# Adding layer 0's bias to the node features by transfers in memory instead of by a matmul in each chunk

## What is computed

```python
h = jnp.maximum(_layernorm(x, axis=-1), 0.0)
x = x + _L0_gnn_ref(h, src, dst, W, b)          # relu(A_norm @ h) @ W.T + b
h = jnp.maximum(_layernorm(x, axis=-1), 0.0)
x = x + _L1_gnn_ref(h, ...)                     # messages with edge types, then a GRU cell
```

## Time and profile before

| | us |
|---|---|
| median of 3 runs | 916.81 (916.66 to 917.4) |
| the profiled execution: its own time | 916.74 |
| the profiled execution: span of its instructions | 915.0 |
| PE busy | 841.8 (92%) |
| DVE busy | 762.6 (83%) |
| ACT busy | 505.8 (55%) |
| POOL busy | 97.1 (11%) |

### The profile page before, as it was taken

The page is one execution under the profiler, slowest core; times in us unless marked ns, Lnnn a source line. Parts: engine busy times, 40 slices in busy tenths (PEclk is TensorE's granted clock), DMA queues, the critical chain, the costliest instruction groups (busy, mean ns, idle before and its releaser), DMA issues.

```text
span 915.0 us, 20961 instructions
## 1 busy us (share of the span) xinstructions
PE 841.8 (92%) x8962; PEld 753.2 (82%) x8962; DVE 762.6 (83%) x934; ACT 505.8 (55%) x940; POOL 97.1 (11%) x86
## 2 busy tenths in 40 slices
PE   2344899999999999999999999999999999999996
PEld 2233788889888888988989888989889888988985
DVE  4987999999999999999999981568766766766886
ACT  3678688888888888888888883211111111111011
POOL 6569202001030020000000000000000000000000
PEclk9999999999999999999999999999999999999999
DMA  4540434346443355443345410497667667667750
GB/s 106 148 168 23 167 147 172 154 179 237 183 174 154 153 205 213 183 163 147 153 180 212 185 30 13 171 293 276 241 254 293 228 246 294 247 228 287 266 207 20
DMA packets 37995, 169.19 MB, mean 185 GB/s; under 512 B 7841, under 2 KB 21036, under 8 KB 34952
## 3 DMA queue, kind: packets, MB, share of 16 engines
q1 hardware_dynamic: 31898, 159.98, 46.5%
q0 software_dynamic: 5664, 6.52, 2.6%
q10 hardware_dynamic: 334, 1.29, 0.5%
HBM read 87.72 MB, written 79.74 MB: 183 GB/s over the span
## 4 chain that ended last, share of the span: by engine, by line
PE 79%; ACT 8%; DVE 6%; POOL 3%; issue 2%; DMA 1%; DVEq 0%; ACTq 0%
PE ps L1357 29%; PE ps L1215 23%; PE ps L1204 14%; ACT ring L1000 6%; POOL tab L525 3%; DVE work L758 2%; PE ps L1241 2%; DVE work L765 1%; PE ps L1227 1%; PE ps L1309 1%; PE ps L1312 1%; PE ps L1314 1%; PE ps L1310 1%; PE ps L1311 1%; PE ps L1313 1%
## 5 line engine op out<-in xcount | busy, mean ns | idle before, releaser
L1204 PE MATMUL ps<-work 128*128 128x106 f16 x3125 | 430.1, 215 | 47.3 <-ACT ring L1000 26.6
L1215 PE MATMUL ps<-ring,tab 125*128 125x250 f16 x2500 | 415.3, 271 | 0.7 <-ACT ring L1005 0.7
L1000 ACT ACTIVATE ring<-ps 128x848 f16<-128x848 f32 x375 | 331.2, 885 | 77.6 <-PE ps L1204 71.1
L1204 PEld LDWEIGHTS ps<-work 128*128 128x128 f16 x3125 | 285.3, 100 | 70.7 <-ACT ring L1000 29.2
L1357 PE MATMUL ps<-ring,tab 125*128 125x250 f16 (+1 forms) x2500 | 277.0, 270 | 0.0
L1357 PEld LDWEIGHTS ps<-ring,tab 125*128 125x128 f16 (+1 forms) x2500 | 242.6, 97 | 28.5
L1215 PEld LDWEIGHTS ps<-ring,tab 125*128 125x128 f16 x2500 | 243.4, 98 | 24.3 <-ACT ring L1005 0.9
L758 DVE TENSOR_TENSOR work<-iota_row,mch 128x3906 f16<-128x3906 f16 x100 | 222.6, 2226 | 4.5 <-PE ps L1204 3.9
L765 DVE TENSOR_TENSOR work<-iota_w,mch 128x3100 f16<-128x3100 f16 x100 | 181.4, 1814 | 0.0
L846 DVE TENSOR_TENSOR work<-work,ring 125x3250 f16<-125x3250 f16 (+1 forms) x92 | 161.7, 1780 | 1.2 <-DMA ring<-adjacency 1.2
L1151 ACT ACTIVATE tab<-ps,bg 128x250 f32<-128x250 f32 x25 | 11.7, 469 | 147.7 <-PE ps L1310 146.9
(11 more groups left out here) (191 smaller groups left out, 636.4 us busy)
## 6 DMA issues: line engine op xcount, KB each, us to landing
adjacency<-ring SPq DMA_DIRECT2D x23, 2937.5 KB
ring<-adjacency SPq DMA_DIRECT2D x46, 812.5 KB, 6.5
ring<-adjacency SPq DMA_DIRECT2D x46, 750.0 KB, 9.4
adjacency<-ring SPq DMA_DIRECT2D x23, 183.1 KB
out<-x_sb SPq DMA_DIRECT2D x24, 125.0 KB
h_turned<-hst SPq DMA_DIRECT2D x23, 125.0 KB, 2.0
tab<-h_turned SPq DMA_DIRECT2D x23, 125.0 KB, 2.1
x_sb<-x SPq DMA_DIRECT2D x3, 560.0 KB
```

The costliest lines, as they stand in the source:

```text
L1000: act.activation(to(x * 2 * u, 2, x), ps[:, s:s + 2, 0:x * SLOTS].rearrange("p b (x h) -> p h b x", h=SLOTS), ACT.Copy).then_inc(sem("evac ...
L1204: last = pe.matmul(ps[:, 2 * (u % 2) + i // BANKW, o:o + WCOLS], lohot[:, s, k, :], combo[:, s, k, :], start=True, stop=True)
L1215: mm = pe.matmul(psD[c % 2], tabv[0][P, h, s, :], adj[c % 2][P, h, :], start=i == 0, stop=i == 2 * BLOCKS - 1)
```

## The change

The bias matmul of each chunk (L1229) goes; the two matmuls by `W` now open and close their own accumulation. `split_bias` (eight DVE instructions) and the memset of its tile on POOL go too. In their place POOL issues, when all of `h0` is made, five transfers that add the bias row from memory to `x_sb` in place, ten blocks (1250 pieces of 512 B, 640 KB) at a time. Each of them waits until the one before has landed. They stand in POOL's queue behind the rows of `h0` and ahead of `run_edges(9)` to `run_edges(24)`. DVE's addition of chunk k now also waits for the transfer that covers its blocks: chunks 0 to 4 for the first, 5 to 9 for the second, and so on. ACT's Sign activation writes into another tile.

```diff
@@ gpsimd_main
-            gp.memset(b_parts[:, :, :], 0.0)
...
                 last.then_inc(sem("rows_p"), 1)
+
+            gp.wait_ge(sem("h0"), ON_ACT)
+            gp.wait_ge(sem("rows_v"), TBATCHES - ON_ACT - ON_POOL)
+            gp.wait_ge(sem("rows_p"), ON_POOL)
+            for t in range(XP):
+                positive(gp, sem("biased"), 16 * t)
+                gp.dma_start(x_sb[P, XB * t:XB * (t + 1), :],
+                             bass.AP(tensor=b0.tensor, offset=b0.offset, ap=[[0, LO], [0, XB], [1, D]]),
+                             accum_op=ALU.add).then_inc(sem("biased"), 16)
             for g in range(3 + RAW, CHUNKS):
                 run_edges(g)
@@ vector_prepare
-            split_bias(v, ch)
@@ post0_x_vector
+            v.wait_ge(sem("biased"), 16 * (CB * k // XB + 1))
             v.wait_ge(sem("psX"), k + 1)
             v.tensor_tensor(x_sb[P, blocks(k), :], psX, x_sb[P, blocks(k), :], ALU.add).then_inc(sem("x1"), 1)
@@ scalar_main
-            act.activation(onesb[:, :], ones[:, 0:LO], ACT.Sign)
+            act.activation(aggr[:, 0:LO], ones[:, 0:LO], ACT.Sign)
@@ post0_x_tensor
-                pe.wait_ge(sem("bias_parts"), 1)
             for j in range(CB):
-                pe.matmul(psX[:, j, :], aggr[:, LO * j:LO * (j + 1)], w0_sb[:, :], start=j == 0, stop=False,
-                          skip_group_check=True)
-            pe.matmul(psX, onesb[0:65, :], b_parts[0:65, :, :], start=False, stop=True, skip_group_check=True)\
-              .then_inc(sem("psX"), 1)
+                last = pe.matmul(psX[:, j, :], aggr[:, LO * j:LO * (j + 1)], w0_sb[:, :], start=True, stop=True)
+            last.then_inc(sem("psX"), 1)
```

More of the change, by code:

```diff
@@ L77 @@
 heads_in weights_in dst_in x_in0 x_in1 x_in2 x_in3 x_in4 ends_set ends_in
-iotas consts consts0 headhots hist totals counted rows_i bias_parts later_in cand_in0 cand_in1 cand_in2 cand_in3 cand_in4 run_i
+iotas consts consts0 headhots hist totals counted rows_i biased later_in cand_in0 cand_in1 cand_in2 cand_in3 cand_in4 run_i
 runs_in0 runs_in1 runs_in2 runs_in3 runs_in4 runs_in5
@@ L191, in gnn @@
         iota_s = sb("iota_s", [128, PAIRS + 1], F16)
-        onesb = sb("onesb", [128, LO], BF16)
-        b_parts = sb("b_parts", [128, CB, D], BF16)
         thr = sb("thr", [128, PAIRS], F32)
@@ L257, in gnn @@
         embf = temps[0:TYPES, :].bitcast(F32)[:, 0:D]
-        bias_high, at = carve(early, at, D)
-        bias_rest, at = carve(early, at, D)
         cand, at = carve(early.bitcast(I32), at, PAIRS, CAND)
@@ L639, in vector_prepare @@
             scale_weights(v, ch)
[L641 to L656, removed]
         def weight_squares(v, ch):
```

## The result

The changed kernel takes **1003.23 us** (1002.62 to 1004.87, four runs) against 917.09 us before it on the same chip (916.66 to 917.4): a ratio of 1.0944, interval 1.093 to 1.0957. That is 86.1 us slower, and far above the range that ended at 945.

The account below looks back on a forecast made before the run. PE and DVE were taken as nearly full in the build loop, PE leading slightly from chunk 3. 916.74 - 2.5 (matmul) - 0 - 0 + 0 = 914.2, median 914.3 us; range 912.8 to 945 us.

Parts of the forecast that it names:

- The matmul: PE's bias matmul removed at 0.11 us per chunk, counted for 23 chunks: 2.5 us saved, between nothing and 3.4.
- Rival 2: DVE holds the build loop, so PE waits for one-hots and nothing is gained: 916.8 us; chance 0.12.
- The splitting: DVE's 2.0 us bias splitting at the start counted as nothing: DVE would wait 3.2 us for first edges instead of 1.2.
- The two deadlines: DVE's chunk 0 addition allows T of 19 us; unpacking chunk 9's edges, fetched behind the fifth transfer, allows about 11.
- T: Time of one bias transfer on POOL's queue from issue to landing, taken as 10.5 us; up to about 11 costs nothing.
- Issuing: POOL's issuing of one 1250-piece transfer: 6.6 us, half of a short fetch's 1.21 us fixed, half growing with pieces.
- Moving the data: Bytes of one transfer, 0.64 MB on 16 engines: about 2.3 us, of which 1 us not covered by issuing.
- low end: Lower bound of one transfer's length: a short fetch's 4.1 us plus 2.3 us for the bytes, 6.4 us.
- High end: Upper bound of one transfer's length: ten times the pieces at POOL's pace, 15.1 us, plus 4.1, 19.2 us.
- Rival 1: Edge fetches come late because issuing 1250 pieces or accumulating is slower: 930 us at T = 15; chance 0.24.
- Rival 3: 125 rows go on 5 engines, bytes take 7.4 us instead of 2.3, T 15.5: 932 us; chance 0.10.
- Rival 4: T above 19.2, perhaps through DVE's traffic, so DVE also stalls in chunk 2: above 947 us; chance 0.06.

Follow-up runs that it names:

- none: Changed kernel without its five transfers and the waits for them, so layer 0's bias is left out of the result: 914.49 us, ratio 0.9973.
- sbuf: Changed kernel with pairs of 112 and 13 rows, three chunks' fetches behind each pair, bias read from its SBUF copy: 914.51 us, ratio 0.9974.
- rowsrc: Changed kernel with pairs of 112 and 13 rows and the bias from SBUF, all fetches still behind the fifth pair: 918.79 us, ratio 1.0019.
- ten: Changed kernel with 112 + 13 rows, fetches moved up, adding ten different pieces of x, each read 125 times, instead of the bias: 913.56 us.
- split: Changed kernel with each transfer cut into a pair of 112 and 13 rows, queue order kept: 967.0 us, ratio 1.0545.
- s125: Changed kernel with only the source moved to the bias copy in SBUF; 125 rows and queue order kept: 991.12 us, ratio 1.0818.
- copy: Changed kernel with three chunks' fetches behind each 125-row transfer, and plain copies overwriting x_sb instead of adding: 937.4 us.
- order: Changed kernel with the edge fetches of three chunks behind each transfer instead of all behind the fifth: 927.76 us, ratio 1.0115.
- both: Changed kernel with pairs of 112 and 13 rows and three chunks' fetches behind each pair, bias still from one memory address: 925.32 us, ratio 1.0079.
- spread: Changed kernel with 112 + 13 rows and fetches moved up, adding 1250 different pieces of x from memory instead of the bias: 913.99 us.

## Why the prediction was wrong

**The matmul: right.** Forecast 2.5 us with the median at 914.3; `none` gave 914.49 and `sbuf` 914.51, so 2.3 and 2.4 us. (The upper bound, 25 x 0.14, is 3.5 us and not 3.4.) The rule used, the distance to the next start and not the 274 ns of the record, is what made it come out. Rival 2, that DVE holds the loop, is out: its waiting for PE shrank from 3.9 to 2.0 us and did not end.

**The splitting: right, as far as it shows.** The 2.3 us are accounted for by the matmul; nothing is left that the splitting would have brought, and in `none` DVE waits the 3.2 us that were forecast.

**The two deadlines: right, and the fetches' place is what costs.** I gave as the rule that from T = 11 us each us costs four. At the 32.0 us that the transfers lay apart that is 4 x (32.0 - 11) = 84 us, and the trace has 75.3, but the two are near each other partly by luck: the terms behind them are off in both directions. The fifth transfer was issued at 220.57 instead of 140, 80.6 us late (my sum had added 7 us for stores, which the 32.0 already hold). Its issuing took 4.0 us and not 6.6. The three fetches took 24.4 us and not 12 to 15. So they landed at 249.0 instead of 159 to 162, 87 to 90 us late. DVE's own need had moved from 159.25 to 248.98 - 75.34 = 173.64, most of it by its first wait of 13.2 us, and 75.3 us are left. One step failed here too: I let DVE be 3.4 us late without loss, and `rowsrc` shows that there is no such room, since its 4.1 us of waiting cost 4.3.

**T: the step that failed.** I bounded T by 6.4 and 19.2 us and took 10.5; it was 25.3 to 34.5. By terms:
- Issuing: reckoned 6.6 us, and 15.1 at the high end; measured 3.63 to 3.82. This was the part I had feared, and it was too high.
- Moving the data: reckoned 2.3 us, of which 1 beside the issuing; measured nearly all of T. The 2.3 us came from POOL's queue, 6.52 MB in 2.6% of the engines' span. But the packets that the trace lists for that queue are of two kinds: those of 4128 and 4608 B carry 6.2 of the 6.52 MB, and nearly all others are of 4 to 16 B. So the rate was that of large packets. One of 4608 B took 231 ns on average, 20 B per ns; one of the 512 B pieces in `ten` took 69 ns, 7.5 B per ns. From the 69 ns, 1250 pieces are 5.4 us of 16 engines' time and 17 of five, an estimate; with rows and source as good as any run had them (`ten`), the data of one pair flowed for 4.6 us, twice the 2.3. The best T seen, 6.8, is just above my low end.
- The two causes that lift it from there are the shared address (T 18.0 to 27.6 in `split`, whose rows are good) and the 125 rows (T 19.7 to 37.2 in `s125`, whose source is good).
- "High end" was therefore no bound: it stretched the issuing tenfold, and left the data at 2.3 us with the same rate and free choice of engines. A bound had to let the dearest unknown, the engines' time for a piece, be as bad as the rows allow, and the earlier trace rows, 5.1 to 10.3 us with the longest beside a store, showed that a store can double it.

**The rivals.** Rival 1 had the right place, the late fetches, and the wrong reasons: issuing was faster than I took it, and adding isn't what makes T long, since `ten` adds as well and lands in 6.8 us. Rival 3, fewer engines, was right in kind and got 0.10, at T = 15.5. The run nearest to it is `s125`: 19.7 us in a clear stretch. It was priced from the same 2.3 us (7.4 us on 5 engines). From the 4.6 us of `ten` it would have been 4.6 x 16 / 5 = 14.7 us of flow, and `s125` has 15.2; that they lie so close is partly luck, since the pair of `sbuf`, which has the source of `s125`, flows for 5.9 us, which would make 18.8.

Against rival 3 I had held that the edge fetches have 125 rows too and land in 5.1 to 10.3 us. They were no evidence against it. The trace doesn't name engines, but it lists each packet's size. The 25 edge fetches before are 40 packets of 4608 B (three rows) and 5 of 1536 B (one row) each. That fits five shares of 25 rows, eight packets of three rows and one of one, and not sixteen shares of 7 or 8 rows: the fetches go in five shares themselves, and are quick with few large packets. A transfer of `copy`, 155 packets of 4096 B and 5 of 1024 B, likewise fits five shares of 250 pieces (31 x 8 + 2). For the adding transfer five shares are inferred: its packets are all of one piece, but never more than 11 are under way at once, against 29 in `ten` (counted over the trace's packets). The count also shows 2750 extra packets of 8 B for each 125-row transfer of the kernel after, and 30 for a pair in `ten`; in `s125` they fall in the stretch of 38 GB/s and are over in that of 58. What they are is open, so how much of the cost of 125 rows is engines and how much these packets is open too.

The Trainium skill (DMA: Bandwidth & Descriptors, the section on why a DMA increments its semaphore by 16) has the divisor rule and, as an exception, direct copies from GpSimd seen on 16 engines. The traces side with the rule: 19.7 to 37.2 us for 125 rows, 7.3 to 15.7 for 112 + 13, all else alike. The exception didn't hold for the adding transfer, nor, by the sizes of its packets, for the plain one of `copy`. I had let the exception decide the forecast.

Rival 4 has the right place (DVE at the first addition, 13.2 us) and a time above 947 us, with a chance of 0.06, but its reason was wrong: DVE did not hold up the issuing of these transfers (3.63 to 3.82 us each, with DVE at work or idle). Here the Trainium skill (SBUF — State Buffer, Who interferes with whom) agrees with the trace. The same section says one thing more that I had left out: a tensor_tensor with both inputs in SBUF contends with GpSimd's reads of SBUF. The indirect fetches read their row numbers (`run_i`) there, and one took 5.86 us beside the one-hots in `rowsrc` and 4.28 us before, against 1.2 us with DVE idle in the kernel after; whether that is the reason, no run tested.

**In no rival:** the shared address. The change's text says it plainly, two strides of 0 over a source of 512 B in memory, and none of the profile's rows bears on it; I wrote only "each read from two places". It makes T 18 to 28 us even with 112 + 13 rows.

**What the causes are worth**, by single repairs of the changed kernel: the place in the queue 75 us (`order`), the rows 36 (`split`), the source 12 (`s125`). They don't add: rows and source work through the same T, and the place sets how often T counts. All three give 88.7 us back, and with them the change is a gain of 2.4 us.

## What to carry to other kernels

Price a transfer of many small pieces by a transfer of like pieces and by the engines that can share it, not by its queue's average rate; cut 125 rows into 112 and 13, and read a broadcast row from SBUF or from several addresses. An in-order queue multiplies a transfer's length by the number of times it waits there: put what others need early (here the fetches) between such transfers, not behind them. When bounding a cost that the trace doesn't show, stretch each of its factors, not only the one that seems dear.

## What the runs showed of the hardware that I had not expected

- 1250 reads of one 512 B address moved at 44 GB/s, of ten addresses at about 160, both to the same rows on the same queue.
- 1250 pieces can be added in place in 6.8 us (`ten`). Issuing an adding transfer of 125 rows takes 3.8 us, a plain copy 2.0.
- A packet of 4608 B took 231 ns, one of 512 B 69 ns (kernel before and `ten`): nine times the bytes for 3.4 times the time.
- A transfer of small pieces takes longer beside stores of large ones: in `s125` 19.7 us alone and up to 37.2 beside them. Stores suffer as well: ACT waited 2.9 us for one in `split` and 4.2 in `copy`, and never before.
- PE can stop while 1250 reads go to one address. In `both`:

```profile
295.49 0.37 PE L1203 MATMUL ps<-ring,tab 125*128 125x250 f16 x1 [4.38 <-issue]
```

It waited for no semaphore that the trace names, and went on some 21 us after the fifth pair had been issued (274.30). `copy` has such a stop of 4.7 us and `split` one of 1.7; `spread`, `ten` and `sbuf` have none above 0.4 us, but neither have `order` and the kernel after, which read one address too. That PE's own instructions come late from memory would fit, but no run tested it, and the one packet of the instruction queue within the stop took 0.96 us, as elsewhere: the cause is open.
- The clock falls when PE stands still and is low for a while after. In the kernel after (us, engines in order, clock, DMA share, GB/s):

```profile
222.00:245.00 23.00, 0.00 (x0) 0.00 (x0) 0.00 (x0) 0.00 (x0) 9.60 (x7) 0.50 0.52 70
246.00:262.00 16.00, 7.34 (x63) 6.19 (x64) 12.95 (x15) 4.69 (x9) 0.00 (x0) 0.56 0.03 9
```

The granted clock was 0.50, the lower level of 1.2 GHz, while PE did nothing. PE went on at 254.66, and over the whole of the second stretch the clock was 0.56. Here it cost nothing that shows: DVE was busy for 12.95 of these 16 us and never waited for PE, and the account closes within 0.3 us. In `both`, where DVE waited for PE behind the stop, the same low clock cost some 2.5 us.
